# A graph network kernel on one core: single slots moved from the end of each edge walk into four places

## The chip, the cores and the metric

The kernel runs on one core of one Trainium2 chip. The metric is the device time of one execution in microseconds (us). Three executions of the kernel before took 3234.87, 3237.06 and 3237.46 us; the median is 3237.06 us.

## The reference, cut to what matters

The input is a graph of 6250 nodes with 256 features each and 106,250 directed edges, sorted by destination. Two graph attention layers run over the edges; a linear attention and a mixture of eight experts follow.

```python
h = (x @ W).reshape(n, heads, out_ch)            # layer 1: 8 heads of 64, layer 2: 1 head of 256
e = leaky_relu(a_src[src] + a_dst[dst], 0.2)     # one logit per edge and head
p = exp(e - m[dst])                              # m: a bound or the largest logit of the node
denom = segment_sum(p, dst)
out = segment_sum(h[src] * (p / denom[dst])[..., None], dst)
# x1 = x + layer2(elu(layer1(norm(x)))) + linear_attention(norm(x));  result = x1 + experts(norm(x1))
```

## The kernel before, in words

Nodes are cut into 49 tiles of 128. Edges are cut into **slots** of 128; a slot's edges are summed into one tile of nodes. Two neighbouring slots make a **pair** (`GROUPS` = 416 pairs, 832 slots) that belongs to one tile. Where the sorted edges pass from a tile to the next, a further **single slot** (`CROSS` = 48 of them) takes the same 128 edges for the other tile. `SRC` and `DST` hold sources and destinations of the 880 slots as columns; `TK` holds the tile of each of the 464 sums (416 of pairs, 48 of single slots).

An **edge walk** goes over the slots in **batches** of four, 220 batches. A batch of pairs has two sums, so two additions to `ACC`; a batch of single slots has four. `steps_of(n)` says which: batches 0 to 207 hold pairs, 208 to 219 (the last 12) single slots. `walk` is layer 1 (table rows of 520 floats), `walk2` is layer 2 (258 floats), with the linear attention spread over its batches by `schedule` and `MIX`.

For each batch n, over a ring of six buffers:

- GpSimd (`fetch`, L716 and L1221) issues four indirect DMAs that gather 128 table rows each. It first waits for the indices, and for the sums of batch n-6 (`summed`), because they free the buffer.
- ScalarE (`stage`, `copy_turned`, `weigh`, `scale_last`) writes the indices of batch n+6, copies a transposed one-hot, takes the exponential, and in layer 1 scales the fourth slot (L759).
- TensorE (`turn`, `spread_nodes`, `sum_up`) transposes the one-hot, spreads node values to edges, and sums: L834 in layer 1, L1429 in layer 2. The sums go to two halves of PSUM in turn (`j` is 0 or 1); a sum waits until the addition before the last has emptied its half (`merged`).
- VectorE (`step`) scales rows (L916) or one-hots (L1617), adds each sum to `ACC` (`merge`: L928, L1626), makes the logits of batch n+2 (`logits`: L897 to L907, L1601 to L1611) and the one-hots of batch n+4. The first logit operation waits for the gathered rows; the last (L907, L1611) runs once per batch, so it serves below as a clock of the batches.

Order is that of each engine's program; semaphores link the engines. Each engine runs most batches in hardware loops with a body of six batches (`tiles`, `turns`, `places`), in walk 2 from batch 116 to 187 with a body of twelve; the rest is straight code. After walk 1 comes `between` (begins with L1886), after walk 2 `deliver` (begins with L2102), then `experts`.

Of the kernel before, what the change touches and what calls it, by code (L numbers as in the profile page):

```python
# [23 lines left out]
P = 128  # L24
# [13 lines left out]
assert PG * KT == GROUPS and PG <= P and GROUPS % 2 == 0 and CROSS % 4 == 0  # L38
# [50 lines left out]
def steps_of(n):  # L89
# [6 lines left out]
def sums_after(n):  # L96

    return steps_of(n)[-1][0] + 1
# [121 lines left out]
def front(nc, allocator, dev):  # L220
# [7 lines left out]
    with ExitStack() as st:  # L228
# [185 lines left out]
        def _(dve):  # L414
# [57 lines left out]
            def ends():  # L472
                dve.wait_ge(ends_in, 16)
                edge_.link(dve.tensor_scalar(tile_i[:, :], last_i[:, :], 7, None, ALU.arith_shift_right))
                dve.tensor_copy(tile_f[:, :], tile_i[:, :]).then_inc(tiles_ready, 1)
                dve.tensor_copy(TK[:, 0:GROUPS], tile_i[:, :].rearrange("a (g h) -> a g h", h=2)[:, :, 0])
# [29 lines left out]
            def edge_rows(k):  # L506
                dve.wait_ge(edge_turned, k + 1)
                part = slice(2 * k * PG, 2 * (k + 1) * PG)
# [108 lines left out]
def walk(nc, allocator, dev, layer, table, AD, ADM, SELF, ACC, arena=None):  # L617
# [10 lines left out]
    with ExitStack() as st:  # L628
# [79 lines left out]
        @block.gpsimd  # L708
        def _(pool):
            def fetch(n, r):  # L710
                pool.wait_ge(staged, n + 1)
                if not isinstance(n, int) or n >= RING:
                    pool.wait_ge(summed, sums_after(n - RING))
# [84 lines left out]
        def _(pe):  # L798
# [11 lines left out]
            def spread_nodes(n, r, t=None):  # L810
                t = tiles_of(pe, n) if t is None else t
# [3 lines left out]
                for (_, j, slots), at in zip(steps_of(n), t):  # L815
# [21 lines left out]
            def step(n, r):  # L837
                t, mine = tiles_of(pe, n + 2), steps_of(n)
                for step_ in mine[:len(mine) // 2]:
                    sum_up(n, r, *step_)  # L840
                spread_nodes(n + 2, (r + 2) % RING, t)
# [22 lines left out]
            spread_nodes(0, 0)  # L864
            turn(2, 2)
            spread_nodes(1, 1)
            step(0, 0)
            for n, r in tiles(pe, 1, PAIRED - 2, RING):
                step(n, r)
            for n in range(PAIRED - 2, NB - 3):  # L870
                step(n, n % RING)
            spread_nodes(NB - 1, (NB - 1) % RING)
# [5 lines left out]
        def _(dve):  # L878
# [56 lines left out]
            def step(n, r, q, hots=True, more=True):  # L935
                scale(n + 1, (r + 1) % RING, 0)
                if not isinstance(n, int) or n > 0:
                    merge(*steps_of(n - 1)[-1][:2])
                scale(n + 1, (r + 1) % RING, 1)
                for k, j, _ in steps_of(n)[:-1]:  # L940
                    merge(k, j)
# [25 lines left out]
            with dve.If(dve.value_load(wide[0:1, 0:1], min_val=0, max_val=1) > 0):  # L967
# [26 lines left out]
                for k, _ in tiles(dve, 0, GROUPS, 1):  # L994
                    largest(k, (2 * k, 2 * k + 1))
                for v, _ in tiles(dve, 0, CROSS, 1):
                    largest(v + GROUPS, (v + 2 * GROUPS,))
# [17 lines left out]
            step(0, 0, 0)  # L1015
            for n, r, q in turns(dve, 1, PAIRED, RING):
                step(n, r, q)
            for n in range(PAIRED, NB - 4):
                step(n, n % RING, n // RING)
            for n in (NB - 4, NB - 3):  # L1020
                step(n, n % RING, n // RING, hots=False)
            step(NB - 2, (NB - 2) % RING, 0, more=False)
            for k, j, _ in steps_of(NB - 2)[-1:] + steps_of(NB - 1):
                merge(k, j)


class At:


    def __init__(self, loop, step, base):  # L1030
        self.loop, self.step, self.base = loop, step, base

    @property
    def fixed(self):
        return self.loop is None

    @property
    def n(self):
        return self.base if self.fixed else self.loop * self.step + self.base

    def back(self, k):
        return At(self.loop, self.step, self.base - k)

    def slot(self, ring):
        assert self.fixed or self.step % ring == 0
        return self.base % ring

    def round(self, ring):
        assert self.fixed or self.step % ring == 0
        return self.base // ring if self.fixed else self.loop * (self.step // ring) + self.base // ring  # L1050

    def among(self, count):
        return not self.fixed or 0 <= self.base < count


def places(eng, first, last, unroll):

    whole = (last - first) // unroll
    if whole > 1:
        with eng.Fori(0, whole) as i:  # L1060
            for u in range(unroll):
                yield At(i, unroll, first + u)
        first += whole * unroll
    for n in range(first, last):
        yield At(None, unroll, n)
# [22 lines left out]
def walk2(nc, allocator, dev, table, AD, ADM, SELF, ACC, XR, rings):  # L1088
# [12 lines left out]
    with ExitStack() as st:  # L1101
# [112 lines left out]
        def _(pool):  # L1214
            def fetch(n, r):
                pool.wait_ge(staged, n + 1)
                if not isinstance(n, int) or n >= RING:
                    pool.wait_ge(summed, sums_after(n - RING))
# [14 lines left out]
            for n, r in tiles(pool, RING, PAIRED, RING):  # L1233
                fetch(n, r)
            for n in range(PAIRED, NB):
                fetch(n, n % RING)
# [164 lines left out]
        def _(pe):  # L1401
# [10 lines left out]
            def spread_nodes(n, r, t=None):  # L1412
                t = tiles_of(pe, n) if t is None else t
# [3 lines left out]
                for (_, j, slots), at in zip(steps_of(n), t):  # L1417
# [14 lines left out]
            def step(b, mixing=None, a=None):  # L1432
                n, r, h = b.n, b.slot(RING), b.slot(HOT)
                t, mine = tiles_of(pe, n + 2), steps_of(n)
                for step_ in mine[:len(mine) // 2]:
                    sum_up(n, r, *step_)
                spread_nodes(n + 2, (r + 2) % RING, t)
# [132 lines left out]
            spread_nodes(0, 0)  # L1570
            turn(2, 2, 2)
            spread_nodes(1, 1)
# [7 lines left out]
            spread_nodes(NB - 1, (NB - 1) % RING)  # L1580
# [5 lines left out]
        def _(dve):  # L1586
# [41 lines left out]
            def step(b, hots=True, more=True):  # L1628
                n, r = b.n, b.slot(RING)
                scale(n + 1, (r + 1) % RING, 0)  # L1630
                if not b.fixed or n > 0:
                    merge(*steps_of(n - 1)[-1][:2])
                scale(n + 1, (r + 1) % RING, 1)
                for k, j, _ in steps_of(n)[:-1]:
                    merge(k, j)
# [110 lines left out]
            with dve.If(dve.value_load(wide[0:1, 0:1], min_val=0, max_val=1) > 0):  # L1746
# [20 lines left out]
                for k, _ in tiles(dve, 0, GROUPS, 1):  # L1767
                    largest(k, (2 * k, 2 * k + 1))
                for v, _ in tiles(dve, 0, CROSS, 1):
                    largest(v + GROUPS, (v + 2 * GROUPS,))  # L1770
# [718 lines left out]
```

## Time and profile before

| | us |
|---|---|
| median of 3 runs | 3237.06 |
| profiled execution | 3236.97 |
| its span, first to last instruction | 3235.1 |
| around the span | 1.9 |
| granted TensorE clock over the span | 0.920 of full |

An execution has a front (to about 137 us), walk 1 (its first gather starts at 138.1 us), `between`, walk 2 (first gather at 1498.9 us), `deliver`, and `experts` from about 2757 us. A row of the profile gives line, engine, operation, what it writes and reads, the count, busy time and mean of one, then the engine's idle time ahead of these instructions and what ended it. "issue" is idle time with no wait that the profile shows.

### The profile page before, as it was taken

To read this page: it belongs to the slowest core of one execution; us is meant where nothing else is said; L and a number is where in the kernel's file an instruction comes from. 1 tells how busy PE (TensorE), PEld (TensorE's weight loads), DVE (VectorE), ACT (ScalarE), POOL (GpSimd) and SP (SyncE) were. 2 spreads that over 40 slices of the span, in tenths; PEclk is the share of its full clock that TensorE was granted. 3 is DMA by queue.
4 is the path that set the end of the run, shared out by engine and by line. 5 is a ranking of instruction groups with operands and counts; after the bars stand their busy time and mean duration, and the time that the engine had idled before them with its cause. 6 is when DMAs were issued, how large, how long until landed. Compare 5 with 4: busy or idle time off the path is not lost. (4 is left out here: it accounts for less than half of the span.)

```text
span 3235.1 us, 72226 instructions
## 1 busy us (share of the span) xinstructions
PE 2657.0 (82%) x16531; PEld 2051.6 (63%) x16532; DVE 2424.6 (75%) x7804; ACT 1260.5 (39%) x4575; POOL 1939.2 (60%) x1978
## 2 busy tenths in 40 slices
PE   6688888888888887476888887777778775899997
PEld 5577777777777775365666665565555545567675
DVE  6798888888888887896766666678778766346555
ACT  3455555555555554133333222444444125121211
POOL 0267777777777775873777777777777716011111
PEclk9899999999999999788999998989889755899999
DMA  6467777777777775343446736433333328232320
GB/s 186 146 186 209 210 208 209 207 209 208 208 207 208 208 210 156 108 106 98 132 132 209 230 105 186 106 106 105 105 106 106 106 69 279 88 114 72 113 77 11
DMA packets 217427, 488.98 MB, mean 151 GB/s; under 512 B 47565, under 2 KB 97241, under 8 KB 217258
## 3 DMA queue, kind: packets, MB, share of 16 engines
q0 software_dynamic: 119696, 367.15, 40.7%
q1 hardware_dynamic: 82782, 106.04, 10.5%
q10 hardware_dynamic: 14780, 13.93, 1.3%
q8 instruction: 60, 0.98, 0.1%
q14 instruction: 109, 0.89, 0.1%
HBM read 427.70 MB, written 64.16 MB: 152 GB/s over the span
## 5 line engine op out<-in xcount | busy, mean ns | idle before, releaser
L716 POOL DMA_INDIRECT w_G<-table,w_idx x880 | 857.0, 974 | 348.6 <-issue 255.6
L1221 POOL DMA_INDIRECT weights<-table,w_idx x880 | 839.8, 954 | 314.2 <-issue 247.3
L834 PE MATMUL PS<-w_G,w_S 128*128 128x260 f32 x3520 | 878.7, 392 | 129.8 <-DVE ACC L928 110.9
L834 PEld LDWEIGHTS PS<-w_G,w_S 128*128 128x128 f32 x3520 | 634.5, 190 | 232.8 <-issue 135.6
L1429 PE MATMUL PS<-weights 128*128 128x257 f32 x1760 | 540.7, 440 | 133.7 <-DVE ACC L1626 66.5
L1429 PEld LDWEIGHTS PS<-weights 128*128 128x128 f32 x1760 | 340.9, 215 | 247.3 <-issue 173.4
L916 DVE TENSOR_TENSOR w_G<-w_G 128x512 f32<-128x512 f32 x660 | 436.6, 690 | 21.7 <-ACT w_G L748 6.9
L759 ACT ACTIVATE w_G<-w_G 128x64 f32<-128x64 f32 x1760 | 441.2, 335 | 0.0
L928 DVE TENSOR_TENSOR ACC<-ACC,PS 128x520 f32 x464 | 320.2, 690 | 18.8 <-PE PS L834 18.8
L1251 ACT ACTIVATE w_PW<-w_Z 128x4 f32<-128x4 f32 x220 | 45.2, 205 | 713.2 <-DVE w_Z L1611 713.1
L2388 POOL DMA_INDIRECT out<-Oe,who x64 | 62.9, 983 | 415.0 <-DVEq L2440 411.8
L1617 DVE TENSOR_SCALAR weights<-iota_row,DST,w_PW 128x128 f32<-128x128 f32 x880 | 274.1, 365 | 31.6 <-issue 20.1
L1626 DVE TENSOR_TENSOR ACC<-ACC,PS 128x257 f32 x464 | 196.5, 423 | 123.6 <-issue 73.7
L748 ACT ACTIVATE w_G<-w_Z 128x32 f32<-128x32 f32 x220 | 50.4, 229 | 537.4 <-DVE w_Z L907 537.4
L1420 PEld LDWEIGHTS PS<-w_parts,w_ST 128*128 128x128 bf16 x2640 | 138.2, 98 | 187.4 <-issue 156.5
L881 DVE TENSOR_SCALAR w_S<-iota_row,DST 128x128 f32<-128x128 f32 x880 | 255.4, 307 | 0.0
L1420 PE MATMUL PS<-w_parts,w_ST 128*128 x2640 | 167.9, 168 | 97.0 <-ACT w_ST L1247 90.8
L1591 DVE TENSOR_SCALAR weights<-iota_row,DST 128x128 bf16<-128x128 f32 x880 | 245.0, 310 | 0.5 <-issue 0.3
L2379 ACT ACTIVATE HT<-PS,weights 128x465 f32<-128x465 f32 (+1 forms) x128 | 85.6, 669 | 367.3 <-PE PS L2344 367.3
L2355 PE MATMUL PS<-weights,HT 128*128 128x256 f32 (+1 forms) x1024 | 222.3, 379 | 0.0
L2344 PE MATMUL PS<-XT,weights 128*128 128x465 f32 (+1 forms) x512 | 214.0, 579 | 0.8 <-DVE XT L2400 0.8
L2355 PEld LDWEIGHTS PS<-weights,HT 128*128 128x128 f32 (+1 forms) x1024 | 189.0, 185 | 31.1 <-issue 0.4
(335 smaller groups left out, 3870.1 us busy)
## 6 DMA issues: line engine op xcount, KB each, us to landing
xbuf<-XR SPq DMA_DIRECT2D x8, 2064.0 KB, 27.6
weights<-in_L_ffn_w SPq DMA_DIRECT2D x16, 1024.0 KB, 9.9
XB<-xbuf SPq DMA_DIRECT2D x7, 2064.0 KB, 9.0
w_G<-table,w_idx POOLq DMA_INDIRECT x880, 3.7
weights<-table,w_idx POOLq DMA_INDIRECT x880
table<-row SPq DMA_DIRECT2D x49, 260.0 KB, 2.0
HR<-table SPq DMA_DIRECT2D x49, 260.0 KB, 2.9
table<-row ACTq DMA_DIRECT2D x49, 129.0 KB, 2.3
```

What stands on the lines that cost most here:

```text
L716: pool.indirect_dma_start(G[:, r, b, :], None, table, IndexOn(ap=idx[:, r, b:b + 1], axis=0)).then_inc(fetched[r], 16)
L759: last = act.activation(feat, feat, ACT.Copy, scale=G[:, r, B - 1, w:w + 1])
L834: last = pe.matmul(PS[:, 2 * j + a, 0:W // layer.banks], lhsT, rhs, start=b == slots[0], stop=b == slots[-1])
L881: last = dve.tensor_scalar(S[:, r, b, :], iota_row[:, :], DST[:, bass.ds(n * B + b, 1)], None, ALU.is_equal)
L916: last = dve.tensor_tensor(feat, feat, one(row[:, :, 4 * C1:], 3, C1), ALU.mult)
L928: dve.tensor_tensor(acc, acc, PS[:, 2 * j:2 * j + 2, 0:HALF], ALU.add).then_inc(merged, 1)
L1221: pool.indirect_dma_start(G[:, r, b, :], None, table, IndexOn(ap=idx[:, r, b:b + 1], axis=0)).then_inc(fetched[r], 16)
L1420: last = pe.matmul(PS[:, 6 + r % 2, b * 2:(b + 1) * 2], ST[:, r % 2, b, :], parts[:, i, bass.ds(at, 1), :].rearrange("p a b -> p (a b)"), ...
L1429: last = pe.matmul(PS[:, 2 * j, 0:W], SW[:, r % 2, b, :], G[:, r, b, 1:1 + W], start=b == slots[0], stop=b == slots[-1])
L1591: last = dve.tensor_scalar(S[:, h, b, :], iota_row[:, :], DST[:, bass.ds(n * B + b, 1)], None, ALU.is_equal)
L1617: last = dve.tensor_scalar(SW[:, r % 2, b, :], iota_row[:, :], DST[:, bass.ds(n * B + b, 1)], PW[:, r, b, :], ALU.is_equal, ALU.mult)
L2355: last = pe.matmul(PS[0:rows_of(j), 4 + j % 4, 0:D], HT[:, f, j * P:j * P + rows_of(j)], w2[:, u, f, :], start=f == 0, stop=f == KF - 1)
```

## The change

The 48 single slots are spread: the walk has four blocks, each of 104 pairs (52 batches) followed by 12 single slots (3 batches). A block is 55 batches; single slots lie in batches 52 to 54, 107 to 109, 162 to 164 and 217 to 219. `SRC`, `DST` and `TK` are laid out in that order, so the copies in the front write them with strides. The tiles and sums are the same; only the order of additions differs.

A hardware loop can't hold both kinds of batch, so `places` cuts the loops. In walk 1 one loop of 34 rounds (33 on GpSimd) becomes four loops of 8 rounds, over batches 1 to 48, 56 to 103, 111 to 158 and 166 to 213 (on GpSimd each stands for the fetch six batches later). Between them are seven batches of straight code. In walk 2 TensorE, VectorE and ScalarE lose one of seven rounds of the loop from batch 10, and the loop of twelve from 116 to 187 (6 rounds) becomes two, 116 to 151 (3 rounds) and 166 to 189 (2 rounds), with 152 to 165 straight. GpSimd's loops in walk 2 are as in walk 1. The instructions of a step are the same.

```diff
-PAIRED = GROUPS // 2
+VPB = CROSS // KT
+PAIRED, ALONE = PG // 2, VPB // 4
+BLOCK = PAIRED + ALONE
...
+def places(eng, first, last, unroll):
+    turning = {c for k in range(KT) for c in (BLOCK * k + 1, BLOCK * k + PAIRED - 3)}
+    cuts = [first] + sorted(c for c in turning if first < c < last) + [last]
+    for lo, hi in zip(cuts, cuts[1:]):
+        whole = (hi - lo) // unroll
+        if whole > 1 and 1 <= lo % BLOCK and hi - 1 - lo // BLOCK * BLOCK < PAIRED - 3:
+            with eng.Fori(0, whole) as i:
+                for u in range(unroll):
+                    yield At(i, unroll, lo + u)
+            lo += whole * unroll
+        for n in range(lo, hi):
+            yield At(None, unroll, n)
...
-    if isinstance(n, int) and n >= PAIRED:
-        return [(GROUPS + 4 * (n - PAIRED) + b, b % 2, (b,)) for b in range(4)]
-    return [(2 * n + j, j, (2 * j, 2 * j + 1)) for j in range(2)]
+    k, i = divmod(b.base, BLOCK)
+    if i >= PAIRED:
+        assert b.fixed
+        return [((PG + VPB) * k + PG + 4 * (i - PAIRED) + v, v % 2, (v,)) for v in range(4)]
+    return [(2 * b.n + (PG + VPB - 2 * BLOCK) * k + j, j, (2 * j, 2 * j + 1)) for j in range(2)]
...
-                dve.tensor_copy(SRC[:, 2 * GROUPS:], PS[:, 6, 0:CROSS])
-                dve.tensor_copy(DST[:, 2 * GROUPS:], PS[:, 6, CROSS:2 * CROSS])
-                dve.tensor_copy(TK[:, GROUPS:], PS[0:1, 7, 0:CROSS])
+                dve.tensor_copy(by_block(SRC[:, :])[:, :, 2 * PG:], by_block(PS[:, 6, 0:CROSS]))
+                dve.tensor_copy(by_block(DST[:, :])[:, :, 2 * PG:], by_block(PS[:, 6, CROSS:2 * CROSS]))
+                dve.tensor_copy(by_block(TK[:, :])[:, :, PG:], by_block(PS[0:1, 7, 0:CROSS]))
...
-            for n, r in tiles(pool, RING, PAIRED, RING):
-                fetch(n, r)
-            for n in range(PAIRED, NB):
-                fetch(n, n % RING)
+            for b in places(pool, 0, NB - RING, RING):
+                fetch(b.n + RING, b.slot(RING), b)
...
-            for n, r, q in turns(dve, 1, PAIRED, RING):
-                step(n, r, q)
-            for n in range(PAIRED, NB - 4):
-                step(n, n % RING, n // RING)
+            for b in places(dve, 0, NB - 4, RING):
+                step(b)
```

## Rows read from the trace of the kernel before

**Rows 1.** The page: busy tenths of the span in 40 slices, 80.9 us each.

```profile
POOL 0267777777777775873777777777777716011111
PEclk9899999999999999788999998989889755899999
```

**Rows 2.** Costliest groups by line: the gathers, and the first logit operation in walk 1.

```profile
L716 POOL DMA_INDIRECT w_G<-table,w_idx x880 | 857.0, 974 | 348.6 <-issue 255.6 <-ACT w_idx L736 77.4 <-PE PS L834 15.3
L1221 POOL DMA_INDIRECT weights<-table,w_idx x880 | 839.8, 954 | 314.2 <-issue 247.3 <-ACT w_idx L1241 53.2 <-PE PS L1429 13.7
L897 DVE TENSOR_TENSOR w_Z<-w_G,PS 128x32 f32<-128x32 f32 x220 | 41.1, 187 | 106.8 <-DMA w_G<-table,w_idx 102.6 <-PE PS L818 3.9
```

**Rows 3.** Windows, L716 alone: start:end, length, busy (count), clock, DMA share, GB/s.

```profile
300.00:1160.00 860.00, 655.26 (x673) 1.00 0.75 208
```

**Rows 4.** Windows, L907 alone (once per batch): catching up, steady, single slots.

```profile
199.10:247.70 48.60, 1.94 (x11) 1.00 0.76 211
300.00:1160.00 860.00, 34.41 (x168) 1.00 0.75 208
1231.30:1287.90 56.60, 1.42 (x8) 1.00 0.57 156
```

**Rows 5.** Lines in 1231.3 to 1287.9 us, single slots: VectorE's additions.

```profile
L928 DVE TENSOR_TENSOR ACC<-ACC,PS 128x520 f32 x32 | 22.2, 693 | 10.5 <-PE PS L834 10.5
```

**Rows 6.** Timeline of walk 1: batch 200's fetch and logit; 219's fetch, logits of 218, 219.

```profile
1169.40 1.00 POOL L716 DMA_INDIRECT w_G<-table,w_idx  x1 [0.30 <-issue]
...
1178.01 0.17 DVE L907 TENSOR_SCALAR w_Z<-w_Z 128x32 f32<-128x32 f32 x1
...
1266.69 0.97 POOL L716 DMA_INDIRECT w_G<-table,w_idx  x1 [0.30 <-issue]
...
1287.64 0.18 DVE L907 TENSOR_SCALAR w_Z<-w_Z 128x32 f32<-128x32 f32 x1
...
1296.24 0.18 DVE L907 TENSOR_SCALAR w_Z<-w_Z 128x32 f32<-128x32 f32 x1
```

**Rows 7.** Timeline of walk 2: fetch and logit of batches 180, 200, then 215, 219.

```profile
2404.45 0.94 POOL L1221 DMA_INDIRECT weights<-table,w_idx  x1 [0.30 <-issue]
...
2423.05 0.17 DVE L1611 TENSOR_SCALAR w_Z<-w_Z 128x4 f32<-128x4 f32 x1
...
2505.48 0.95 POOL L1221 DMA_INDIRECT weights<-table,w_idx  x1 [0.30 <-issue]
...
2512.89 0.17 DVE L1611 TENSOR_SCALAR w_Z<-w_Z 128x4 f32<-128x4 f32 x1
...
2602.62 0.17 DVE L1611 TENSOR_SCALAR w_Z<-w_Z 128x4 f32<-128x4 f32 x1
2603.00 1.19 POOL L1221 DMA_INDIRECT weights<-table,w_idx  x1 [1.80 <-issue]
...
2630.06 0.17 DVE L1611 TENSOR_SCALAR w_Z<-w_Z 128x4 f32<-128x4 f32 x1
```

**Rows 8.** Windows, L1611 alone: batches 131 to 190, 191 to 199, 210 to 218.

```profile
2164.50:2470.30 305.80, 12.65 (x60) 0.91 0.39 105
2470.30:2508.20 37.90, 1.63 (x9) 1.00 0.40 107
2560.00:2623.60 63.60, 1.49 (x9) 0.53 0.29 80
```

**Rows 9.** Windows, L1221 alone, the same stretch of the queries.

```profile
2164.50:2470.30 305.80, 231.95 (x243) 0.91 0.39 105
```

**Rows 10.** Timeline of walk 2: a late gather; VectorE after one round of the loop of twelve.

```profile
1762.28 0.16 DVE L1601 TENSOR_TENSOR w_Z<-weights,PS 128x4 f32<-128x4 f32 x1 [4.76 <-DMA weights<-table,w_idx]
...
2160.60 0.35 DVE L1617 TENSOR_SCALAR weights<-iota_row,DST,w_PW 128x128 f32<-128x128 f32 x1 [3.97 <-issue]
```

**Rows 11.** Windows: PE, PEld, DVE, ACT, POOL busy (count), clock, DMA share, GB/s.

```profile
2640.00:2760.00 120.00, 64.77 (x352) 61.52 (x352) 80.37 (x259) 54.89 (x114) 49.49 (x50) 0.51 0.70 225
```

**Rows 12.** Lines in the front: the copies of the single slots' columns.

```profile
L515 DVE CAST SRC<-PS 128x48 int32<-128x48 f32 x1 | 0.2, 199 | 0.0
```

More of the change, by code:

```diff
@@ L86, in ring4, with __init__, fixed, n @@
     yield from tiles(eng, 4, TILES, 4)
-def steps_of(n):
-    if isinstance(n, int) and n >= PAIRED:
-        return [(GROUPS + 4 * (n - PAIRED) + b, b % 2, (b,)) for b in range(4)]
-    return [(2 * n + j, j, (2 * j, 2 * j + 1)) for j in range(2)]
-def sums_after(n):
-    return steps_of(n)[-1][0] + 1
+class At:
+    def __init__(self, loop, step, base):
+        self.loop, self.step, self.base = loop, step, base
+    @property
+    def fixed(self):
+        return self.loop is None
+    @property
+    def n(self):
+        return self.base if self.fixed else self.loop * self.step + self.base
+    def back(self, k):
+        return At(self.loop, self.step, self.base - k)
+    def slot(self, ring):
+        assert self.fixed or self.step % ring == 0
+        return self.base % ring
+    def round(self, ring):
+        assert self.fixed or self.step % ring == 0
+        return self.base // ring if self.fixed else self.loop * (self.step // ring) + self.base // ring
+    def among(self, count):
+        return not self.fixed or 0 <= self.base < count
+def places(eng, first, last, unroll):
[10 more added lines that the diff above has]
+            yield At(None, unroll, n)
+def steps_of(b):
+    b = At(None, 1, b) if isinstance(b, int) else b
+    k, i = divmod(b.base, BLOCK)
[3 more added lines that the diff above has]
+    return [(2 * b.n + (PG + VPB - 2 * BLOCK) * k + j, j, (2 * j, 2 * j + 1)) for j in range(2)]
+def sums_after(b):
+    return steps_of(b)[-1][0] + 1
 class Chain:
@@ L507, in edge_rows @@
                 dve.wait_ge(edge_turned, k + 1)
-                part = slice(2 * k * PG, 2 * (k + 1) * PG)
+                part = slice(4 * BLOCK * k, 4 * BLOCK * k + 2 * PG)
                 ps = PS[:, 6 + k % 2, 0:4 * PG].rearrange("p (a h k) -> p a h k", a=2, h=2)
@@ L709, in _, with fetch @@
         def _(pool):
-            def fetch(n, r):
+            def fetch(n, r, before=None):
                 pool.wait_ge(staged, n + 1)
-                if not isinstance(n, int) or n >= RING:
-                    pool.wait_ge(summed, sums_after(n - RING))
+                if before is not None:
+                    pool.wait_ge(summed, sums_after(before))
                 pool.sem_inc(released, 1)
@@ L808, in turn, with spread_nodes @@
                 last.then_inc(turned, 1)
-            def spread_nodes(n, r, t=None):
-                t = tiles_of(pe, n) if t is None else t
+            def spread_nodes(b_, t=None):
+                n, r = b_.n, b_.slot(RING)
+                t = tiles_of(pe, b_) if t is None else t
                 pe.wait_ge(st_ready, n + 1)
@@ L814, in spread_nodes @@
                     pe.wait_ge(z_ready, n - 1)
-                for (_, j, slots), at in zip(steps_of(n), t):
+                for (_, j, slots), at in zip(steps_of(b_), t):
                     for b in slots:
@@ L835, in sum_up, with step @@
                 last.then_inc(summed, 1)
-            def step(n, r):
-                t, mine = tiles_of(pe, n + 2), steps_of(n)
+            def step(b):
+                n, r = b.n, b.slot(RING)
+                t, mine = tiles_of(pe, b.back(-2)), steps_of(b)
                 for step_ in mine[:len(mine) // 2]:
                     sum_up(n, r, *step_)
-                spread_nodes(n + 2, (r + 2) % RING, t)
+                spread_nodes(b.back(-2), t)
                 for step_ in mine[len(mine) // 2:]:
@@ L863, in _ @@
             pe.wait_ge(parts_ready, 1)
-            spread_nodes(0, 0)
+            spread_nodes(At(None, RING, 0))
             turn(2, 2)
[L866 to L872, printed above, removed]
+            spread_nodes(At(None, RING, 1))
+            for b in places(pe, 0, NB - 3, RING):
+                step(b)
+            spread_nodes(At(None, RING, NB - 1))
             for n in range(NB - 3, NB):
@@ L931, in merge, with step @@
                     dve.tensor_tensor(acc, acc, PS[:, 2 * j, 0:W], ALU.add).then_inc(merged, 1)
-            def step(n, r, q, hots=True, more=True):
+            def step(b, hots=True, more=True):
+                n, r, q = b.n, b.slot(RING), b.round(RING)
                 scale(n + 1, (r + 1) % RING, 0)
                 if not isinstance(n, int) or n > 0:
-                    merge(*steps_of(n - 1)[-1][:2])
+                    merge(*steps_of(b.back(1))[-1][:2])
                 scale(n + 1, (r + 1) % RING, 1)
-                for k, j, _ in steps_of(n)[:-1]:
+                for k, j, _ in steps_of(b)[:-1]:
                     merge(k, j)
@@ L992, in largest @@
                     xown_.closed(len(slots) * per)
[L994 to L997, printed above, removed]
+                for c in range(KT):
+                    for k, _ in tiles(dve, 0, PG, 1):
+                        largest(k + (PG + VPB) * c, (2 * k + 4 * BLOCK * c, 2 * k + 4 * BLOCK * c + 1))
+                    for v, _ in tiles(dve, 0, VPB, 1):
+                        largest(v + (PG + VPB) * c + PG, (v + 4 * BLOCK * c + 2 * PG,))
             bound_.link(dve.tensor_copy(ADM[:, :, 0:H], AD[:, :, H:2 * H]))
@@ L1014, in _ @@
             scale(0, 0, 1)
-            step(0, 0, 0)
-            for n, r, q in turns(dve, 1, PAIRED, RING):
-                step(n, r, q)
-            for n in range(PAIRED, NB - 4):
-                step(n, n % RING, n // RING)
+            for b in places(dve, 0, NB - 4, RING):
+                step(b)
             for n in (NB - 4, NB - 3):
-                step(n, n % RING, n // RING, hots=False)
-            step(NB - 2, (NB - 2) % RING, 0, more=False)
+                step(At(None, RING, n), hots=False)
+            step(At(None, RING, NB - 2), more=False)
             for k, j, _ in steps_of(NB - 2)[-1:] + steps_of(NB - 1):
                 merge(k, j)
[L1027 to L1065, printed above, removed]
 MIX = {"prepare": (2, 0, 1, 3), "keys": (5, TILES, 1, 5), "context": (59, 2 * (TILES // 4), 1, 5), "fold": (88, 0, 1, 5),
@@ L1214, in _, with fetch @@
         def _(pool):
-            def fetch(n, r):
+            def fetch(n, r, before=None):
                 pool.wait_ge(staged, n + 1)
-                if not isinstance(n, int) or n >= RING:
-                    pool.wait_ge(summed, sums_after(n - RING))
+                if before is not None:
+                    pool.wait_ge(summed, sums_after(before))
                 pool.sem_inc(released, 1)
@@ L1232, in _ @@
                     pool.indirect_dma_start(XG[:, :], None, table, IndexOn(ap=xidx[:, 0:1], axis=0)).then_inc(xfetched, 16)
[L1233 to L1236, printed above, removed]
+            for b in places(pool, 0, NB - RING, RING):
+                fetch(b.n + RING, b.slot(RING), b)
         @block.scalar
@@ L1410, in turn, with spread_nodes @@
                 last.then_inc(turned, 1)
-            def spread_nodes(n, r, t=None):
-                t = tiles_of(pe, n) if t is None else t
+            def spread_nodes(b_, t=None):
+                n, r = b_.n, b_.slot(RING)
+                t = tiles_of(pe, b_) if t is None else t
                 pe.wait_ge(st_ready, n + 1)
@@ L1416, in spread_nodes @@
                     pe.wait_ge(z_ready, n - 1)
-                for (_, j, slots), at in zip(steps_of(n), t):
+                for (_, j, slots), at in zip(steps_of(b_), t):
                     for b in slots:
@@ L1631, in step @@
                 if not b.fixed or n > 0:
-                    merge(*steps_of(n - 1)[-1][:2])
+                    merge(*steps_of(b.back(1))[-1][:2])
                 scale(n + 1, (r + 1) % RING, 1)
-                for k, j, _ in steps_of(n)[:-1]:
+                for k, j, _ in steps_of(b)[:-1]:
                     merge(k, j)
@@ L1765, in largest @@
                     xown_.closed(len(slots) * 5)
[L1767 to L1770, printed above, removed]
+                for c in range(KT):
+                    for k, _ in tiles(dve, 0, PG, 1):
+                        largest(k + (PG + VPB) * c, (2 * k + 4 * BLOCK * c, 2 * k + 4 * BLOCK * c + 1))
+                    for v, _ in tiles(dve, 0, VPB, 1):
+                        largest(v + (PG + VPB) * c + PG, (v + 4 * BLOCK * c + 2 * PG,))
             bound_.link(dve.tensor_copy(ADM[:, :, 0:1], AD[:, :, 1:2]))
```

16 lines of the change are left out of this document (9 added, 7 removed).

## The prediction

> **What bounds the kernel now.** I read the page's slices first, then the costliest lines, then windows over one line of each engine, then the timeline at single batches.
>
> In the slices GpSimd is at 7 tenths all through both walks, and it is the only engine at the same digit in both [rows 1]. The lines say what that is: 880 gathers per walk, 974 and 954 ns each [rows 2]. Each has an idle 0.30 us ahead of it that waits for nothing the profile shows [rows 6], so a batch of four costs GpSimd 4 x (0.974 + 0.30) = 5.10 us in walk 1. The window agrees: 673 gathers in 860 us are 5.11 us per batch, and the logits, once per batch, come 168 times in the same 860 us, 5.12 us [rows 3, 4]. VectorE waits for the gathered rows in nearly every batch of walk 1, 102.6 us in all [rows 2]. So the paired part of walk 1 is paced by GpSimd's issue of gathers. The other engines can go faster: just after the start, with rows in stock, 11 batches take 48.6 us, 4.42 us each [rows 4].
>
> I use one number for the state of the pipeline, the **lag**: from the start of a batch's first gather to its last logit operation. At its floor (rows used as soon as they land) it is 1178.01 - 1169.40 = 8.6 us in walk 1 and 2512.89 - 2505.48 = 7.4 us in walk 2 [rows 6, 7].
>
> The 12 batches of single slots are another regime: 8 batches take 56.6 us, 7.08 us each [rows 4]. The additions wait 10.5 us for TensorE there [rows 5]; twice as many sums pass through the same two halves of PSUM. GpSimd doesn't slow down, so the lag grows to 1296.24 - 1266.69 = 29.5 us for the last batch [rows 6]. Walk 2 ends alike: 9 batches in 63.6 us, 7.1 us each, and a last lag of 2630.06 - 2603.00 = 27.1 us [rows 8, 7]. After GpSimd's last fetch nothing runs beside this backlog. That is what the change touches.
>
> **The change part by part.**
>
> *Walk 1, the end.* Batch 218 is made in the step of a paired batch (logits run two batches ahead), so it is at the floor: logit at fetch of 218 + 8.6 = fetch of 219 - 5.1 + 8.6. Batch 219's logit is one single-slot step later, 7.08 us: fetch of 219 + 10.6 us. Now it is + 29.5, so 18.9 us go. Bound from the other side: the last such step took 1296.24 - 1287.64 = 8.6 us [rows 6], which leaves 17.4. What follows the last logit is unchanged. I take 18.5 us.
>
> *Walk 1, three groups of three single batches inside.* Each such batch takes 7.08 against GpSimd's 5.12, 1.96 us over; a group adds 5.9 us and lifts the lag from 8.6 to 14.5. This costs nothing if GpSimd never stops and the surplus is worked off before the next group. It stops when the buffer of batch n-6 isn't free. Rows 7 show the one place where that happens: batch 219's gather starts after 1.80 us idle (0.30 is usual), 0.38 us after the logit of batch 215. So GpSimd is held once the lag passes about 4 x 5.1 - 0.4 = 20 us. 14.5 is below. Working off goes at 5.12 - 4.42 = 0.70 us per paired batch: 9 of the 52 that follow. Cost 0; if that cover were gone, 5.9 us per group.
>
> *Walk 2, the end.* Same form: 218 at the floor, 7.4 - 5.03 = 2.4 us after the fetch of 219, plus 7.1 is 9.5 us, against 27.1: 17.6 us. Also the hold of 1.5 us (1.80 - 0.30) before batch 219's gather goes [rows 7], since the lag is far under 20. Together 19.1 us.
>
> *Walk 2, group at 52 to 54.* It falls where SyncE's stores into xbuf share the DMA engines: one gather came 4.76 us late [rows 10]. VectorE waits there anyway, so part of the group's surplus fills that wait. Later batches work it off as in walk 1. Cost 0.
>
> *Walk 2, groups at 107 to 109 and 162 to 164.* Here the cover is thin, since VectorE, ScalarE and TensorE also carry the attention's queries. 60 batches take 305.8 us, 5.10 us each [rows 8], while GpSimd issues 243 gathers, 5.03 per batch [rows 9]: the lag drifts up instead of down and is 2423.05 - 2404.45 = 18.6 us at batch 180 [rows 7], near the 20 us limit. A single-slot batch at the stretch's clock isn't in the trace. The two further additions alone, bounded by walk 1's wider ones of 693 ns [rows 5], would be 1.4 us; the end's 7.1 us, at half clock, against a free pace of 37.9 / 9 = 4.2 us [rows 8] would be 2.9. I take the 2.0 of walk 1. What is given back: the loop of twelve loses its round ends after batches 151 and 163, and behind a round's end VectorE stood still 3.97 us on issue [rows 10]; two of these are 7.9 us. So the highest lag becomes 18.6 + 6 - 7.9 = 16.7, plus what is left of the group at 107, between 0 and 6: 17 to 23 us. Over 20, GpSimd is held by the rest: 0 to 3 us, and up to 10 if single slots cost 3 each there and nothing is worked off. I take 2 us. From batch 191 on the pace is 4.2 against 5.03, 0.8 us per batch over 26 batches, 21 us: any lag is gone before the end, but a hold of GpSimd stays in the end time. So walk 2 gives 19.1 - 2 = 17.1 us.
>
> The Trainium skill, "Runtime: NRT & Kernel Launch", section "Instruction fetch mechanics", says that instructions are prefetched strictly in order and that a taken branch whose target has left the small instruction window costs a fetch stall. The 3.97 us on issue behind the long loop's end agrees. By that rule fewer long rounds and more straight code favour VectorE in walk 2, as counted above from the row; the same rule has a bad side on GpSimd, which is the third rival below.
>
> *Front.* The three copies of the single slots' columns get strided targets; 199 ns now for one of 48 columns [rows 12]. Under 1 us even if each doubled. 0.
>
> *After the walks.* The granted clock is 0.51 in the 120 us behind walk 2 with TensorE busy for 64.8 of them [rows 11], so it could gain if the clock stayed up over the shorter end. At most half of 64.8; I take 0, as the last paired batches before it aren't at full clock either, and keep up to 8 us for the range.
>
> **Sum**: 18.5 + 17.1 = 35.6 us off the profiled execution's 3236.97 (span 3235.1 + 1.9), which equals the median of 3237.06 within 0.1. Forecast 3202 us.
>
> **Rivals.**
>
> 1. *The ring fills in the queries.* The mechanism works elsewhere, but GpSimd is held by 6 to 10 us instead of 2: gain 28 to 32, time 3205 to 3209. For it: 18.6 us of lag already [rows 7] and 5.10 against 5.03. Against: two round ends less.
>
> 2. *The groups are paid in place.* If a single-slot batch stops the gathers too, the nine inner batches of each walk cost 9 x 1.96 + 9 x 2.05 = 36 us and the end's gain is eaten: 3202 + 36 = 3238, no change. For it: the slack is only 0.70 us per batch. Against: in walk 1 even the last batch's gather, behind eleven single-slot batches, starts after no more than the usual 0.30 us [rows 6], so the gathers don't stop for such batches.
>
> 3. *GpSimd stalls on its own code* (slower). It now has four loops per walk instead of one and straight code between. If its loop rounds stalled as VectorE's did, 3.97 us [rows 10], nothing would hide it, for GpSimd sets the pace. 28 round ends per walk would be 2 x 28 x 3.97 = 222 us, time 3424; it takes the nine first to undo the gain of 35.6, so it decides from five stalls per walk. Against: GpSimd passes 33 round ends in walk 1 now, and its idle per gather stays near 0.30 (860 us less 655.26 busy, over 673 gathers) [rows 3]; its body is six fetches, far shorter than VectorE's twelve steps. The skill's rule just named is what would make it so, for a body that crosses the window.
>
> 4. *More than forecast.* TensorE's clock stays up through the shorter ends and into what follows: 5 to 8 us more, 3194 to 3197.
>
> **How the numbers follow.** Forecast 0.70, rival 1 0.13, rival 4 0.06, rival 2 0.06, rival 3 0.05. The forecast's own spread is 17.4 to 18.9 in walk 1 and 16 to 19 in walk 2, 3199 to 3204. With rival 1 and 4 and the unknown cost of a single slot in the queries the range is 3193 to 3212. A measurement of this kernel tells about 0.2% (6.5 us) from no change. Faster by more than that: 0.70 + 0.13 + 0.06 = 0.89; within: 0.06; slower: 0.05.
>
> **What would show it.** In the windows of the logits the walks' last batches should come at the paired pace up to batch 218, and the last lag should be 10 to 12 us in walk 1 and 9 to 11 in walk 2. Walk 1 should end about 18 us earlier and the start of walk 2 move by the same; walk 2's end by 33 to 36. GpSimd's gathers should keep 5.11 us per batch over the groups of walk 1, with idle 0.30. In the queries the greatest lag should lie between 17 and 21, and any idle over 0.30 of GpSimd's there is rival 1. Three humps of about 6 us in walk 1's lag, gone after about nine batches, prove the absorption. The prediction is wrong if GpSimd idles on "issue" at the new loops' entries, if the inner groups stretch GpSimd's own interval, or if a round of VectorE's loops in walk 1 now begins with a wait on issue.

## The result, and the profile after

Four executions each: before 3237.26 us median (3234.87 to 3239.92), changed 3199.18 us (3198.12 to 3202.6). The ratio is 0.9884, 95% interval 0.9867 to 0.9901: faster by 38 us. Forecast were 3202 us and a range of 3193 to 3212. The profiled execution of the changed kernel took 3202.6 us (span 3200.9), 34.4 less than the profiled one before. It is the slowest of its four, so the trace can explain 34 of the 38 us.

The experiments fell on different chips. In eight of the twelve the kernel before took 3897 to 3945 us, in the other four 3236; so each is read by its ratio.

The page of the changed kernel, busy tenths in 40 slices of 80.0 us. Inside the walks GpSimd stays at 7 tenths as before [rows 1]:

```profile
POOL 0267777777777776873777777777777735011111
PEclk9889999999999999788999897889989865899999
```

The gathers and the first logit operation by line (count | busy us, mean ns | idle before, what ended it) answer to [rows 2]. They cost the same:

```profile
L769 POOL DMA_INDIRECT w_G<-table,w_idx x880 | 855.2, 972 | 351.1 <-issue 256.9 <-ACT w_idx L787 74.3 <-PE PS L886 19.6
L1229 POOL DMA_INDIRECT weights<-table,w_idx x880 | 840.3, 955 | 315.5 <-issue 251.5 <-ACT w_idx L1247 50.6 <-PE PS L1436 13.4
L947 DVE TENSOR_TENSOR w_Z<-w_G,PS 128x32 f32<-128x32 f32 x220 | 40.9, 186 | 93.5 <-DMA w_G<-table,w_idx 89.1 <-PE PS L870 3.9
```

VectorE's wait for rows in walk 1 fell from 102.6 to 89.1 us: the single-slot batches use part of that slack up. The timeline at the ends of both walks (start, us, engine, line) answers to [rows 6, 7]: for each walk the last batch's first gather, its last logit operation, and the first operation of the stage behind the walk:

```profile
1267.68 0.95 POOL L769 DMA_INDIRECT w_G<-table,w_idx  x1 [0.30 <-issue]
...
1279.24 0.18 DVE L957 TENSOR_SCALAR w_Z<-w_Z 128x32 f32<-128x32 f32 x1
...
1290.37 0.26 DVE L1894 TENSOR_TENSOR RD<-ACC,SELF 128x96 f32<-128x96 f32 x1 [0.32 <-PEq L681]
...
2586.34 0.95 POOL L1229 DMA_INDIRECT weights<-table,w_idx  x1 [0.31 <-issue]
...
2595.80 0.17 DVE L1618 TENSOR_SCALAR w_Z<-w_Z 128x4 f32<-128x4 f32 x1
...
2604.96 0.24 DVE L2110 TENSOR_TENSOR rstd<-ACC,SELF 128x49 f32<-128x49 f32 x1 [0.33 <-PEq L1109]
```

The last lag is 1279.24 - 1267.68 = 11.6 us in walk 1, where it was 29.5, and 9.5 in walk 2, where it was 27.1. In the trace before, the operations at 1290.37 and 2604.96 stand at 1307.37 and 2639.22, so they come 17.0 us earlier, then 34.3. `between` is 1.2 us shorter (its start to walk 2's first gather, 190.3 us against 191.5). Behind walk 2 nothing changed.

Windows over L957 alone (start:end, length, busy (count), clock, DMA share, GB/s), in walk 1: the first group of three single-slot batches, then the nine behind it.

```profile
428.60:448.70 20.10, 0.52 (x3) 1.00 0.75 208
448.70:489.80 41.10, 1.63 (x9) 1.00 0.75 209
```

Single slots take 20.1 / 3 = 6.7 us, the pairs behind them 41.1 / 9 = 4.57, while GpSimd needs 5.1: a hump that rises by 5 and is worked off in nine batches. In walk 1 the lags after the three inner groups peak at 13.5, 13.6 and 14.5 us, and over all three GpSimd's idle ahead of a gather stays at 0.30.

Windows over L1618 alone in walk 2: the groups at 107 and at 162, batches 191 to 199, and 210 to 218 (pairs now, except the work for 217):

```profile
2033.00:2049.90 16.90, 0.49 (x3) 0.80 0.40 109
2311.60:2331.20 19.60, 0.48 (x3) 0.84 0.39 105
2452.40:2493.90 41.50, 1.70 (x9) 1.00 0.39 106
2543.60:2588.80 45.20, 1.70 (x9) 0.85 0.41 107
```

Nine batches there took 63.6 us before [rows 8]; the last row has 45.2, 5.02 each: GpSimd's pace.

Two rows show what was lost. First, walk 2's first group: the logit of batch 56, and GpSimd held ahead of batch 60.

```profile
1784.10 0.17 DVE L1618 TENSOR_SCALAR w_Z<-w_Z 128x4 f32<-128x4 f32 x1
...
1784.06 0.97 POOL L1229 DMA_INDIRECT weights<-table,w_idx  x1 [2.63 <-issue]
```

Batch 56's gather began at 1761.69, so its lag is 22.4 us, and GpSimd idles 2.63 instead of 0.30. Second, VectorE's first operation after the skipped slow path (the exact largest logit, which this input doesn't need), in both walks:

```profile
160.31 0.38 DVE L1050 COPY ADM<-AD 128x392 f32<-128x392 f32 x1 [4.63 <-issue]
...
1496.24 0.19 DVE L1779 COPY ADM<-AD 128x49 f32<-128x49 f32 x1 [3.73 <-issue]
```

Before the change these were 1.58 and 1.27 us. The change wrote that path's two loops four times, once per block, which the section on the change doesn't mention.

### The profile page after: what moved, and what is told of

It reads as the page before. It is cut to its first block and busy times, and to the rows that moved or that the text cites. A ratio compares the mean times of both kernels' runs of the same rounds, so it can differ in the third digit from the quotient of the medians.

```text
span 3200.9 us, 71778 instructions
## 1 busy us (share of the span) xinstructions
PE 2646.5 (83%) x16531; PEld 2049.6 (64%) x16532; DVE 2412.8 (75%) x7804; ACT 1260.2 (39%) x4575; POOL 1938.1 (61%) x1978
## 5 line engine op out<-in xcount | busy, mean ns | idle before, releaser
L769 POOL DMA_INDIRECT w_G<-table,w_idx x880 | 855.2, 972 | 351.1 <-issue 256.9
L1257 ACT ACTIVATE w_PW<-w_Z 128x4 f32<-128x4 f32 x220 | 45.2, 205 | 694.8 <-DVE w_Z L1618 694.6
```

## The experiments

**1. The order alone.** Both kernels keep the changed code but put all 12 single-slot batches last; the second also has no loop of twelve in walk 2.

```diff
-VPB = CROSS // KT
-PAIRED, ALONE = PG // 2, VPB // 4
-BLOCK = PAIRED + ALONE
+ALONE = (0, 0, 0, 12)              # single-slot batches after each block of 52 paired ones
+PAIRED = PG // 2
+FIRST = [PAIRED * k + sum(ALONE[:k]) for k in range(KT)]
...
-        if whole > 1 and 1 <= lo % BLOCK and hi - 1 - lo // BLOCK * BLOCK < PAIRED - 3:
+        if whole > 1 and unroll < 12 and any(a + 1 <= lo and hi <= z - 3 for a, z in stretches()):
```

(`unroll < 12` in the second kernel only; `stretches` gives the runs of paired batches.)

> All 12 single-slot batches back at the end of each walk (batches 208 to 219), loops over the batches as before the change, the rest of the code as after it. Theory (the gain is the backlog at the ends): the backlog is back, last lag 29 us in walk 1 and 27 in walk 2. In the profile after the change VectorE stands 4.63 us on issue behind the skipped slow path (its code is four times as long) where it stood 1.58 before; that stays, about 3 us in walk 1. Time 3238 to 3242. Rival (the gain comes from the rewritten column layout, the waits or the slow path's code, not from the order): 3197 to 3210. Rival (skipping the longer slow path costs nothing at the end): 3236 to 3238.

Measured: 3905.51 us against 3900.03, ratio 1.0011 (1.0 to 1.0022). That fits the theory's 3 us, but says little: where before takes 3900 us the changed kernel itself gains only 0.5% (experiment 5).

> Single slots at the end as in the kernel before, all four gathers, but walk 2's loop of twelve batches (116 to 187, six rounds) written as straight code. Where the kernel before takes 3900 us its lag in that stretch is 31 us and GpSimd is held, and 12 batches with a round end take 84.2 us against 78.5 straight, 5.7 us per round end. Theory: five round ends and the exit go, 25 to 34 us, ratio to the kernel before 0.992 to 0.995 with the slow path's code still in; so on such a chip the changed kernel's gain is that of its fewer round ends, not of its order. Rival (the order gives it there too): 0.999 to 1.001. Where the kernel before takes 3237 us: no change, the lag of the queries is worked off before the end.

Measured where before takes 3236 us: 3240.24 us, ratio 1.001 (1.0001 to 1.002). With the single slots at the end nothing is gained by the columns' layout, the waits or the straight code; 3.8 us are lost. So the gain is the order's. Its trace has the slow path's stall:

```profile
L1064 DVE COPY ADM<-AD 128x392 f32<-128x392 f32 x1 | 0.4, 368 | 5.0 <-issue 5.0
```

In the queries its highest lag is 11.6 us against 18.6 before, so straight code does save VectorE's round ends, but GpSimd sets the pace and the time doesn't move. The part of the expectation for a chip at 3900 us wasn't tried.

The 3.8 us can't all be put down to the slow path: in this trace walk 1 starts 1.1 us later than before, and GpSimd is held for 0.7 and 1.0 us ahead of batches 218 and 219 of walk 1, which it wasn't before.

**2. GpSimd's pace taken away.** The first of four gathers only, in the order with the single slots last and in the changed order.

```diff
-                for b in range(B):
+                for b in range(1):
                     pool.indirect_dma_start(G[:, r, b, :], None, table, ...).then_inc(fetched[r], 16)
...
+            pool.memset(G[:, :, :, :], 0.0).then_inc(filled_once, 1)
```

> The order of before (single slots last), but only the first of each batch's four gathers is issued; the other three row buffers are zeroed once at each walk's start and used as they are, so three quarters of the gathered rows are left out. GpSimd then needs 1.25 us per batch and paces nothing; the steps of the other engines are unchanged. Theory: paired batches take 4.4 to 5 us and single ones 7.1 to 8 in both walks; no lag builds up that waits behind GpSimd, since fetches are always six batches ahead. Base for the next kernel.

> The same one gather per batch in the changed order. Theory (the gain is backlog that GpSimd's pace left slack to work off): with no slack the order is worth nothing, so walk 1 from its first logit to its last sum takes as long as with the single slots at the end, within 3 us. In walk 2 the round ends of the long loop are no longer covered by lag; two or three of them go, 8 to 16 us. Rival (single-slot batches are cheaper when spread, whatever sets the pace): walk 1 is 15 to 19 us shorter here as well.

Measured: 2979.29 and 2960.07 us (ratios 0.9205 and 0.9143 to before, 3236.5). Windows from the first to the last logit of a walk, over that line alone: single slots last, walk 1 and walk 2:

```profile
178.90:1172.90 994.00, 37.96 (x219) 0.99 0.21 58
1398.90:2373.50 974.60, 35.41 (x219) 0.93 0.20 60
```

and in the changed order:

```profile
177.70:1172.70 995.00, 37.91 (x219) 0.99 0.21 58
1399.90:2354.90 955.00, 35.43 (x219) 0.94 0.21 61
```

Walk 1 takes 994 and 995 us: without GpSimd's pace the order is worth nothing, so single-slot batches are not cheaper when spread, they are covered. That decides against the rival. In single stretches of walk 1 the three groups cost 8.7, 9.1 and 8.7 us in place and the last 12 batches give 25.3 back.

Walk 2 is 19.6 us shorter, above the 8 to 16 forecast. Between its logits the last 29 batches fall by 24.5 us; the stretches with the first two groups (batches 45 to 66 and 100 to 115) grow by 10.6 and 7.9; batches 115 to 150 fall by 2.7. The 16 batches from 151 to 166 fall from 87.6 to 77.7 us, though three of them are single-slot now and none was before: the two round ends and the looped code there cost more than the group. How the 19.6 us divide among round ends, the clock and the groups is open.

The edit takes three quarters of the gathered bytes away as well, so by itself it doesn't tell GpSimd's issue from the transfers. The rows of the changed kernel do: a gather takes GpSimd 972 ns in walk 1, at a DMA share of 0.75, and 955 ns in walk 2, at 0.39, where a table row is half as long. A batch of four takes 5.1 and 5.0 us alike, so it is the issue that paces.

**3. The slow path's code.**

```diff
-                for c in range(KT):
+                with dve.Fori(0, KT) as c:
                     for k, _ in tiles(dve, 0, PG, 1):
-                        largest(k + (PG + VPB) * c, ...)
+                        largest(c * (PG + VPB) + k, ...)
```

> As changed, but the slow path (skipped in this input) is written as one hardware loop over the four blocks, so that its code is as long as before the change and not four times as long. Theory: VectorE's 4.63 us on issue behind the skipped code in walk 1 falls back to 1.6, and since that stretch holds up GpSimd's seventh batch, 3 us go off the end; walk 2 starts with GpSimd not held, so nothing there. 0.9990 of the changed kernel (3 us less). Rival (the late start is worked off later): 1.000 of the changed kernel.

Measured: 3880.68 us, ratio 0.9957 (0.9943 to 0.9972), beside 0.9952 (0.9935 to 0.9968) of the changed kernel on the same chip. Not told apart there. The stall itself is gone, in both walks:

```profile
L1050 DVE COPY ADM<-AD 128x392 f32<-128x392 f32 x1 | 0.4, 368 | 1.5 <-issue 1.5
L1779 DVE COPY ADM<-AD 128x49 f32<-128x49 f32 x1 | 0.2, 193 | 1.2 <-issue 1.2
```

The same lines had 5.3 and 3.8 us in the changed kernel of that comparison. So the stall's cause is shown to be the length of the skipped code. Its price shows where gathers set the pace: walk 1's seventh batch is first gathered at 177.88 us before, at 180.87 in the changed kernel, and at 178.17 with a compact slow path (experiment 7), some 2.7 us.

**4. The stores into xbuf moved away from the group.**

```diff
             sp.wait_ge(blank_ready, 2)
+            sp.wait_ge(summed, 122)
             for e in range(EXPERTS):
```

> As changed, but SyncE's stores into xbuf in walk 2 wait for the sums of batch 57, so that they no longer meet the first group of single slots (batches 52 to 54). In the profile of the changed kernel GpSimd falls back by 2.3 us between batches 54 and 60 of walk 2. Theory (the group's surplus comes on top of the gathers' late landing and fills the ring): the 2.3 us go, 0.9993 of the changed kernel. Rival (the fall-back comes from the group alone, or from a loop's end there): no change.

Measured: 3882.07 us, ratio 0.996 (0.9945 to 0.9976). GpSimd was held in nearly every batch on that chip, so the 2.3 us couldn't show; inconclusive there. Experiment 7 has the same edit where gathers set the pace.

**5. The same kernel where before takes 3900 us.**

> The changed kernel itself once more, as the base for the others of this comparison. Theory and rivals alike: 0.988 of the kernel before, if this chip's gathers pace the walks as in the first comparison; where another engine paces them (GpSimd held in nearly every batch) the backlog at the end is no longer what costs, and the ratio is 0.993 to 1.000.

Measured: 3878.83 us, ratio 0.9952 (0.9935 to 0.9968). The second case of the expectation: GpSimd is held, its idle ahead of walk 1's gathers is 649.0 us against 351.1, and the excess is ended by TensorE's sums:

```profile
L769 POOL DMA_INDIRECT w_G<-table,w_idx x880 | 877.6, 997 | 649.0 <-issue 261.9 <-PE PS L886 257.1 <-ACT w_idx L787 77.4
```

A batch takes 6.5 us and outside the groups the lag stands near 22 us from batch 12 on. From the first gather to the start of `between`, walk 1 takes 1626.0 - 141.2 = 1484.8 us, and 1624.3 - 136.5 = 1487.8 with the single slots last (experiment 1): 3 us, where the gather-paced chip gave 17. That is what the theory says of a walk without slack behind GpSimd, but this pair doesn't prove it: the two traces are of different chips, and over batches 12 to 50, where the order is the same, they already differ by 7.2 us the other way. The test is experiment 2.

The 0.5% comes from walk 2, which takes 1436.0 us from its first gather to its last logit against 1469.0 with the single slots last. Of the 33 us, 25 lie in batches 115 to 190, where the loop of twelve lost round ends, and 11 behind them. What share the order has in that wasn't tried.

**6. Groups of another size.**

> All 12 single-slot batches in one group in the middle, batches 104 to 115, with pairs only at the end. Theory (the ring absorbs up to a lag of about 20 us, above it GpSimd is held): in walk 1 the group would lift the lag from 8.6 by 12 x 1.96 to 32, so GpSimd is held for about 12 us; the end gives 29.5 - 8.6 = 21 and 2 to 3 us more because the last two batches are pairs; slow path's code 3 us lost. Walk 1: about -9 against before. Walk 2: held about 12, and 0 to 8 more since the queries follow at a high lag; the end gives about 23. Time 3217 to 3225, and GpSimd idle beyond 0.30 us in batches 109 to 119 of both walks. Rival (groups are paid in place from the first batch): held 24 per walk, time 3240 to 3248. Rival (absorbed without a limit): 3192 to 3196.

Measured (`ALONE = (0, 12, 0, 0)`): 3874.4 us, ratio 0.9933 (0.9908 to 0.9958).

> Four single-slot batches after each of the first three blocks, none at the end: batches 52 to 55, 108 to 111, 164 to 167. Theory: the last lag falls from 11.5 to 8.6 us in walk 1 and from 9.5 to 7.4 in walk 2, and the last two batches, now pairs, finish 2 to 3 us sooner in each walk; a group of four reaches a lag of 16.5, under 20, except the first of walk 2, which meets the stores into xbuf and is held 2 us more than after the change. Time 3188 to 3194. Rival (only the number of batches in a row counts, the last three were hidden as well): 3199 to 3202. Rival (groups of four are too long in the queries, GpSimd is held there): 3203 to 3209.

Measured (`ALONE = (4, 4, 4, 0)`): 3876.99 us, ratio 0.9932 (0.9911 to 0.9953).

> Groups of four single-slot batches after blocks 1 to 3, none at the end, once more: in the first comparison of this kernel the kernel before took 3900 us and GpSimd was held in nearly every batch, so it told nothing of a walk that gathers pace. If the kernel before takes about 3237 us here: theory (last lag at its floor, pairs last, slow path's code lost 3 us) 3188 to 3194; rival (the last three single-slot batches were hidden as well) 3199 to 3202; rival (held in the queries by groups of four) 3203 to 3209. If it takes 3900 again: 0.993 as before.

Measured: 3917.32 us against 3944.87, ratio 0.9934 (0.9911 to 0.9956), its last case. Where GpSimd is held anyway one group of twelve does as well as three of four, and both are some 7 us under the changed kernel's 0.9952, with intervals that overlap. The forecasts of these three for a kernel before of 3237 us weren't tested. So the ring's limit for a group of twelve is open where gathers set the pace; that limit rests on the holds at lags above 20 us, 22.4 in the changed kernel and those ahead of the last batches with the single slots last.

**7. A version that beats both.** Experiment 6's three groups of four, the compact slow path (a loop over the three blocks and a tail), and the stores behind batch 57; then also without the loop of twelve.

> Three groups of four single-slot batches and none at the end, the compact slow path, and the stores into xbuf after batch 57. Theory: 8 us from the ends (lag at its floor and pairs last), 3 from the slow path's code, 2 to 4 from the stores: 13 to 15 us less than the changed kernel, 0.9953 to 0.9960 of it. Rival (the last three batches of single slots were hidden already): 5 us less, 0.998.

Measured where before takes 3897 us: 3873.91 us, ratio 0.9936 (0.9917 to 0.9955). That is 4.9 us under the changed kernel there (experiment 5), the rival's 5 and not the theory's 13 to 15; but GpSimd is held there and the intervals overlap, so it decides nothing.

> Three groups of four single-slot batches and none at the end, compact slow path, stores into xbuf after batch 57, and the loop of twelve straight. Theory, where the kernel before takes 3900 us: as the kernel with the first three (0.9936) and another 15 to 20 us for its remaining round ends, 0.989 to 0.991. Where it takes 3237: 0.984 to 0.986, from the ends. Rival (straight code there stalls on its instructions as much as the round ends did): no gain over 0.9936.

Measured where before takes 3236 us: 3187.45 us (3186.51 to 3188.75), ratio 0.9848 (0.9832 to 0.9865), 49 us under before and about 12 under the changed kernel. Its timeline at the same six places:

```profile
1263.26 0.95 POOL L782 DMA_INDIRECT w_G<-table,w_idx  x1 [0.30 <-issue]
...
1272.09 0.18 DVE L970 TENSOR_SCALAR w_Z<-w_Z 128x32 f32<-128x32 f32 x1
...
1281.27 0.26 DVE L1914 TENSOR_TENSOR RD<-ACC,SELF 128x96 f32<-128x96 f32 x1 [0.33 <-PEq L694]
...
2575.02 0.94 POOL L1246 DMA_INDIRECT weights<-table,w_idx  x1 [0.30 <-issue]
...
2583.54 0.17 DVE L1635 TENSOR_SCALAR w_Z<-w_Z 128x4 f32<-128x4 f32 x1
...
2589.38 0.24 DVE L2130 TENSOR_TENSOR rstd<-ACC,SELF 128x49 f32<-128x49 f32 x1 [0.32 <-PEq L1125]
```

Walk 1: the lag is 8.8 us where the changed kernel has 11.6 (2.8 us), what follows the last logit takes 9.2 instead of 11.1 (1.9), and the last gather starts 4.4 earlier, 2.7 of it through the slow path. Walk 2: the last lag is 8.5 instead of 9.5, what follows it takes 5.8 instead of 9.2, and between its first and last gather 2.1 us are gone, the hold of the first group: GpSimd's idle there never exceeds 0.30. So the last three single-slot batches were not hidden. The edits weren't run one by one on this chip.

This trace also prices walk 2's first group apart from the stores, which begin only at 1783.77 here. Windows over the last logit operation: the changed kernel's batches 54 to 56, then this kernel's 54 to 57:

```profile
1760.70:1784.30 23.60, 0.50 (x3) 0.78 1.05 360
1745.10:1777.30 32.20, 0.98 (x4) 0.73 0.41 108
```

These are 23.6 / 3 = 7.9 us per batch beside the stores and 32.2 / 4 = 8.05 without them, against 5.03 for GpSimd: about 3 us of surplus each. The lag goes from 7.4 us at batch 53 to 19.5 at 57, just under the limit, and nothing is held. In the changed kernel the stores had lifted it to 13.8 before the group came. So the stores didn't make the group dearer; they raised the level on which it stood.

## Why the prediction was right, point by point

- *GpSimd's gathers pace both walks*: shown. With three quarters of them gone both walks shrink by 12%, and in walk 1 the order no longer matters.
- *Walk 1's end, 18.5 us*: the lag fell by 18.0 us. The walk ends only 17.0 earlier: its seventh batch started 3.0 us later, and GpSimd won 2.0 back on the way.
- *Walk 1's inner groups cost 0, hump to 14.5, gone after nine batches*: peaks of 13.5, 13.6 and 14.5, nine batches, idle 0.30. Right; a single-slot batch took 6.7 us where 7.08 was assumed, a pair behind it 4.57 where 4.42 was, and the two nearly cancel.
- *Walk 2's end, 19.1 us*: the lag fell by 17.6 and the hold of 1.5 ahead of batch 219 went. Right.
- *Walk 2's group at 52 to 54, cost 0*: wrong. The claim was that the surplus fills the wait for late rows. It came on top: the lag was 13.8 at batch 53 through the stores, the group added 8.6, and at 22.4, over the limit of 20, GpSimd was held for 2.3 us that stayed in the end time. The size was off too: 8.6 us are 2.9 per single-slot batch, where about 2.0 was counted in both walks. With 2.0 the lag would have stopped at about 19.8, at the limit, and next to nothing would have been held. By the prediction's own sign, a group that stretches GpSimd's interval, this place counts against it.
- *Walk 2's groups in the queries, hold of 2 us, highest lag 17 to 21*: wrong the other way. No hold, highest lag 16.0, at batch 144 and so not even behind a group. The surplus was taken as 2.0 us per single-slot batch; the windows give 16.9 / 3 = 5.6 and 19.6 / 3 = 6.5 us against 5.03, so 0.6 and 1.5. The hold forecast here (2 us) and the one that came at the first group (2.3) cancel in the sum by luck.
- *Front and after, 0*: the copies cost nothing visible (walk 1's first gather moves by 0.1 us), but the sum left out a part of the change that it never priced, the slow path written four times: 3 us in walk 1. In walk 2 the like stall of 2.5 us more is covered, because GpSimd has six batches in hand there.
- *The clock behind walk 2, 0*: right, 0.51 over the same 120 us, so the fourth rival is out:

```profile
2605.80:2725.80 120.00, 64.76 (x351) 61.50 (x351) 80.20 (x259) 54.84 (x114) 49.85 (x50) 0.51 0.69 224
```

- *GpSimd stalls on its own code*: no idle over 0.30 us in walk 1 at any of the new loops' ends. The third rival was on the wrong engine; VectorE had the stall, at a skipped branch. The length of the skipped code decided it in walk 1: 1.5 us on issue over the short path, 4.6 to 5.3 over the long one. The Trainium skill, "Runtime: NRT & Kernel Launch", "Instruction fetch mechanics", tells of such a stall for a taken branch out of the prefetched window, and these rows agree; that the idle time is instruction fetch is not shown by the trace itself.

The sum, 35.6 us, stands against 34.4 of the profiled executions: right in total, and in part by luck. The falls of the last lags were counted as 18.5 + 17.6 us and came as 18.0 + 17.6, and the hold of 1.5 us went in both. From that go 2.3 us, held at a place where none was forecast, in the stead of the 2 us that were, and 3 us never counted. The latter were offset by small gains that nobody forecast: 2.0 us of GpSimd's own pace in walk 1 (0.7 were lost in walk 2) and 1.2 us in `between`. Their causes are open. The medians differ by 38.1; what made the changed kernel's profiled execution 3.4 us longer than its median isn't in the trace and stays open.

## What to carry to other kernels

Where one engine paces a pipeline and the others have slack, put the work that is heavy for the others inside the walk, in groups that the ring can hold (surplus per item times items, on top of the lag already there), and end on the lightest items: the end has no slack to hide in. Price the lag and the surplus at the place where each group goes, late transfers included, and look at code that is only skipped. Where the others set the pace, the reordering itself gives nothing: 994 and 995 us in walk 1 with GpSimd relieved.

## What the runs showed of the hardware that wasn't expected

On the chips where before takes 3900 us, ScalarE and VectorE start late on what they wait for from TensorE, as long as GpSimd issues gathers. The timeline of the changed kernel on one of them, at the end of walk 1 (GpSimd's last gather is that at 1594.72):

```profile
1594.13 0.63 PE L858 MATMUL PS<-w_ident,w_S 128*128 128x128 bf16 x4
1594.72 0.96 POOL L769 DMA_INDIRECT w_G<-table,w_idx  x1 [0.30 <-issue]
...
1596.69 0.60 ACT L793 ACTIVATE w_ST<-PS 128x512 bf16<-128x512 bf16 x1 [3.16 <-remote]
1596.74 0.70 DVE L978 TENSOR_TENSOR ACC<-ACC,PS 128x520 f32 x1 [1.89 <-remote]
...
1600.83 0.39 PE L858 MATMUL PS<-w_ident,w_S 128*128 128x128 bf16 x4
1601.26 0.60 ACT L793 ACTIVATE w_ST<-PS 128x512 bf16<-128x512 bf16 x1 [0.83 <-PE PS L858]
```

The transposes end at 1594.76, yet the copy that waits for them starts at 1596.69, 1.0 us after GpSimd's last gather ended, and VectorE's addition with it. With GpSimd idle, the same pair is 0.04 us apart (1601.22 to 1601.26). Over batches 12 to 211 of walk 1 this copy starts 0.75 to 1.25 us behind the end of a batch's four gathers in 133 of 200 cases, and in 6 of 200 where before takes 3237 us (the changed kernel both times). A batch takes 6.5 us there. That TensorE's signals are what comes late is a reading of these rows, not shown by itself. Why some chips do this and the other, whose GpSimd hardly ever pauses, doesn't, is open.
